# Handing every fourth product of a state-space scan from VectorE to GpSimd

## The chip, the cores and the metric

The kernel runs as one program on one core of a Trainium2 chip. The metric is the time of one execution on the device, in microseconds (us), as the median of several runs. In a profile PE is TensorE (PEld its weight loads), DVE is VectorE, ACT is ScalarE, POOL is GpSimd and SP is the queue that starts most transfers.

## What is computed

The whole program is a small network of four blocks. The change touches only the selective scan of the first block. There, after a convolution, every window's positions are walked in four directions, and a recurrence with 16 states runs along each walk:

```python
def step(h, inp):
    u, dt, Bl, Cl = inp
    dA = jnp.exp(dt[..., None] * A)
    h = h * dA + (dt * u)[..., None] * Bl[:, :, None, :]
    y = jnp.einsum('bkdn,bkn->bkd', h, Cl)
    return (h, y)
```

So for each of the 16 states there is a decay `exp(dt * A)`, an input `drive * B` with `drive = dt * u`, a scan over the positions, a product of the scanned state with `C`, and a sum of these products over the states.

## The kernel before

The scan stage takes the work in NU = 64 units: four groups of columns with 16 states (NS) each. A unit is one state on 128 partitions by UC = 1024 columns in f32. The columns hold 16 windows with L positions each. The first position of a window has decay zero, so one scan instruction runs through all windows of a unit. Each engine walks the units in order, in its own loop, and semaphores alone tie the loops together:

- TensorE, in iteration u: it waits for scan u-2 (`scanned`), spreads row n of `b_parts` over the partitions into `p_bb[:, u % 2]` (L510, two bf16 matmuls), waits until ScalarE has emptied `p_cb` (`c_copied`), spreads `c_parts` into `p_cb` (L516, two matmuls), and then adds `hc` of unit u-3 to `p_y` through an identity (L526, two f32 matmuls, four instructions).
- ScalarE: it waits for scan u-2, writes the decays into `d_a[:, u % 2]` (L539, an exponential), waits for `p_cb` and for `hc` of unit u-3, and copies `p_cb` to `cb` (L543).
- VectorE: it waits for the spread B, multiplies `drive` with `p_bb` in place in PSUM (L555), waits for the decays and for `hc` of unit u-3, and scans `d_a` (SBUF) and `p_bb` (PSUM) into `hs` (L560). After the scans of units 17, 33 and 49, and at the end, it reads the finished sum of a group from `p_y` (L550, `read_y`).
- GpSimd: it waits for scan u and the copied C and multiplies `hs` with `cb` into `hc` (L573).

`hs`, `cb` and `hc` are rings of three units (RING). `p_bb` and `d_a` have two slots each, `p_cb` has one, and each of them holds a whole unit. Together `p_bb` (4 banks), `p_cb` (2) and `p_y` (2) fill the PSUM. ScalarE's and VectorE's instructions run strictly in program order, and so do the instructions of TensorE, so a wait holds back all that stands behind it on its engine.

Of the kernel before, what the change touches and what calls it, by code (L numbers as in the profile page):

```python
# [8 lines left out]
ACT = mybir.ActivationFunctionType  # L9
ALU = mybir.AluOpType  # L10
# [11 lines left out]
L = NB * POS  # L22
RANK = 8
BANK = 512
# [33 lines left out]
def build_program(nc, io):  # L58
    with ExitStack() as ctx:
        sig = Signals(nc, ctx)  # L60
        chain_n = {"dve": 0, "act": 0, "pool": 0}

        def sb(name, shape, dt=F32, stack=ctx):
            return stack.enter_context(nc.sbuf_tensor(name, shape, dt))

        def ps(name, shape, dt=F32, stack=ctx):
            return stack.enter_context(nc.psum_tensor(name, shape, dt))
# [112 lines left out]
        with ExitStack() as st:  # L180
            x_tok = sb("x_tok", [128, T // 128, NB, C], stack=st)
            p_x = ps("p_x", [R, T], stack=st)
            with nc.Block() as block:
                @block.sync
                def _(sp):
                    sp.dma_start(ident[:], io["ident"]).then_inc(sig["load_const"], 16)
                    for b in range(NB):
                        sp.dma_start(x_tok[:, :, b, :], io["x"][b].rearrange("(j p) c -> p j c", p=128)).then_inc(sig["load_x"], 16)
                    sp.wait_ge(sig["load_const"], 16)
# [21 lines left out]
        with ExitStack() as st:  # L211
# [9 lines left out]
            drive = sb("drive", [128, 2, NW * L], stack=st)  # L221
            b_parts = sb("b_parts", [96, 2, NW * L], BF16, stack=st)
            c_parts = sb("c_parts", [96, 2, NW * L], BF16, stack=st)
            decay = sb("decay", [128, 2, NS], stack=st)
            pick = sb("pick", [96, NS, 128], BF16, stack=st)
# [260 lines left out]
            with ExitStack() as s2:  # L486
                UC = NW * L // 2
                RING = 3
                p_bb = ps("p_bb", [128, 2, UC], stack=s2)
                p_cb = ps("p_cb", [128, UC], stack=s2)  # L490
                p_y = ps("p_y", [128, UC], stack=s2)
                d_a = sb("d_a", [128, 2, UC], stack=s2)
                hs = sb("hs", [128, RING, UC], stack=s2)
                cb = sb("cb", [128, RING, UC], stack=s2)
                hc = sb("hc", [128, RING, UC], stack=s2)
                NU = 4 * NS
                def unit(u):
                    g, n = divmod(u, NS)
                    return g // 2, (g % 2) * UC, n
                with nc.Block() as block:  # L500
                    @block.tensor
                    def _(pe):
                        for u in range(NU + RING):
                            if u < NU:
                                k, c0, n = unit(u)
                                if u >= 2:
                                    pe.wait_ge(sig["scanned"], u - 1)
                                for h in range(2):
                                    c = slice(c0 + h * BANK, c0 + (h + 1) * BANK)
                                    last = pe.matmul(p_bb[:, u % 2, h * BANK:(h + 1) * BANK], pick[:, n], b_parts[:, k, c], start=True, stop=True)  # L510
                                last.then_inc(sig["b_spread"], 1)
                                if u >= 1:
                                    pe.wait_ge(sig["c_copied"], u)
                                for h in range(2):
                                    c = slice(c0 + h * BANK, c0 + (h + 1) * BANK)
                                    last = pe.matmul(p_cb[:, h * BANK:(h + 1) * BANK], pick[:, n], c_parts[:, k, c], start=True, stop=True)  # L516
                                last.then_inc(sig["c_spread"], 1)
                            if u >= RING:
                                v = u - RING
                                n = v % NS  # L520
                                if n == 0 and v:
                                    pe.wait_ge(sig["y_read"], v // NS)
                                pe.wait_ge(sig["hc"], v + 1)
                                for h in range(2):
                                    c = slice(h * BANK, (h + 1) * BANK)
                                    last = pe.matmul(p_y[:, c], ident[:], hc[:, v % RING, c], start=(n == 0), stop=(n == NS - 1))  # L526
                                last.then_inc(sig["y_summed"], 1)

                    @block.scalar
                    def _(act):  # L530
                        act.wait_ge(sig["first_decay_zero"], 1)
                        for u in range(NU):
                            k, c0, n = unit(u)
                            if u >= 2:
                                act.wait_ge(sig["scanned"], u - 1)
                            src = step[:, k, c0:c0 + UC].rearrange("p (w l) -> p w l", l=L)
                            dst = d_a[:, u % 2].rearrange("p (w l) -> p w l", l=L)

                            act.activation(dst[:, :, 1:L], src[:, :, 1:L], ACT.Exp, scale=decay[:, k, n:n + 1]).then_inc(sig["d_a"], 1)  # L539
                            act.wait_ge(sig["c_spread"], u + 1)  # L540
                            if u >= RING:
                                act.wait_ge(sig["hc"], u - RING + 1)
                            act.activation(cb[:, u % RING], p_cb[:], ACT.Copy).then_inc(sig["c_copied"], 1)  # L543

                    @block.vector
                    def _(dve):
                        def read_y(g):
                            k, c0, _ = unit(g * NS)
                            dve.wait_ge(sig["y_summed"], (g + 1) * NS)
                            dve.scalar_tensor_tensor(y_seq[:, k, c0:c0 + UC], seqf[:, k, c0:c0 + UC], skip[:, k:k + 1], p_y[:],  # L550
                                                     ALU.mult, ALU.add).then_inc(sig["y_read"], 1)
                        for u in range(NU):
                            k, c0, n = unit(u)
                            dve.wait_ge(sig["b_spread"], u + 1)
                            dve.tensor_tensor(p_bb[:, u % 2], drive[:, k, c0:c0 + UC], p_bb[:, u % 2], ALU.mult).then_inc(sig["d_bu"], 1)  # L555
                            dve.wait_ge(sig["d_a"], u + 1)
                            if u >= RING:
                                dve.wait_ge(sig["hc"], u - RING + 1)
                            dve.wait_ge(sig["d_bu"], u + 1)
                            dve.tensor_tensor_scan(hs[:, u % RING], d_a[:, u % 2], p_bb[:, u % 2], 0.0, ALU.mult, ALU.add).then_inc(sig["scanned"], 1)  # L560
                            if u >= NS and u % NS == 1:
                                read_y(u // NS - 1)
                        read_y(3)

                    @block.gpsimd
                    def _(pool):
                        pool.memset(d_a[:], 0.0).then_inc(sig["first_decay_zero"], 1)
                        for u in range(NU):
                            pool.wait_ge(sig["scanned"], u + 1)
                            pool.wait_ge(sig["c_copied"], u + 1)  # L570
                            if u >= RING:
                                pool.wait_ge(sig["y_summed"], u - RING + 1)
                            pool.tensor_tensor(hc[:, u % RING], hs[:, u % RING], cb[:, u % RING], ALU.mult).then_inc(sig["hc"], 1)  # L573

            with ExitStack() as s2:
# [104 lines left out]
def more(nc, io, loc):  # L681
# [613 lines left out]
    with ExitStack() as st:  # L1295
# [27 lines left out]
                 for t in range(4 * h, 4 * h + 4, n) for j in range(4)]  # L1323
        NU, EARLY = len(units), len(units) // 2
        scored = sb("scored", [128, EARLY, BANK], stack=st)
# [635 lines left out]
```

## Time and profile before

| | us |
|---|---|
| median of 3 runs (lowest, highest) | 1204.1 (1201.89, 1204.28) |
| profiled execution, its own time | 1202.41 |
| its span, first to last instruction | 1200.6 |
| the scan stage in it, first scan to end of last `read_y` | 97.65 to 332.36 |

The profiled execution takes 1.8 us more than its span, which lies outside the instructions, and is 1.7 us below the median. Times in the rows are microseconds from the start of the span.
### The profile page before, as it was taken

The page shows a single profiled execution, that of the slowest core. Times are in us where ns is not written, and L with a number is a line of the kernel's source. Part 1 is how long each engine was busy: PE and PEld are TensorE (multiplying, and loading weights), DVE is VectorE, ACT ScalarE, POOL GpSimd, SP SyncE. Part 2 cuts the span into 40 slices and gives each one's busy share as a digit, 9 for nine tenths or more (in the row PEclk, how much of TensorE's full clock was granted, in tenths as well). Part 3 has the DMA queues.
Part 4 walks back from the last instruction along what each step waited for, and adds up shares of the span by engine and source line. Part 5 has one row for each costly group of instructions (what it writes and reads, how often), then busy time and mean ns, then how long its engine had stood idle before and what let it go on. Part 6 is the DMA issues. An engine that isn't in the chain of part 4 may idle for free. (4 is left out here: it accounts for less than half of the span.)

```text
span 1200.6 us, 11335 instructions
## 1 busy us (share of the span) xinstructions
PE 747.2 (62%) x4114; PEld 435.2 (36%) x4114; DVE 479.7 (40%) x828; ACT 454.9 (38%) x1547; POOL 226.0 (19%) x130
## 2 busy tenths in 40 slices
PE   4807777777767655545555555557995555548975
PEld 1302222232233323223333333335773333325753
DVE  5597999999855534500000000012020000018652
ACT  3446556565424422033333333332212333335531
POOL 2276666666600000020000000000000000002200
PEclk9956999999995575555555555555555555555995
DMA  2020000000000000100000000000000000000000
GB/s 61 1 53 1 0 1 0 1 0 1 0 5 1 1 20 9 58 1 1 1 1 1 1 0 1 1 1 1 1 1 1 1 1 1 1 1 1 1 20 10
DMA packets 9570, 7.68 MB, mean 6 GB/s; under 512 B 7154, under 2 KB 8066, under 8 KB 9224
## 3 DMA queue, kind: packets, MB, share of 16 engines
q1 hardware_dynamic: 9512, 6.93, 2.4%
q8 instruction: 33, 0.54, 0.2%
q14 instruction: 25, 0.20, 0.1%
HBM read 5.09 MB, written 0.26 MB: 4 GB/s over the span
## 5 line engine op out<-in xcount | busy, mean ns | idle before, releaser
L791 PE MATMUL L2p_z<-L2yx,L2v 64*32 64x2 f32 x2048 | 267.9, 199 | 242.1 <-ACT L2yx L801 236.3
L801 ACT ACTIVATE L2yx<-L2p_z 32x2 f32<-32x2 f32 x1024 | 165.2, 161 | 389.2 <-PE L2p_z L791 389.2
L791 PEld LDWEIGHTS L2p_z<-L2yx,L2v 64*32 64x32 f32 x2048 | 180.4, 135 | 340.0 <-ACT L2yx L801 316.0
L692 DVE COPY xn<-L2yx 32x512 f32<-32x512 f32 x2 | 0.8, 417 | 431.1 <-ACT L2yx L801 264.2
L573 POOL TENSOR_TENSOR hc<-hs,cb 128x1024 f32<-128x1024 f32 x64 | 150.9, 2358 | 81.6 <-DVE hs L560 81.6
L560 DVE TENSOR_TENSOR_SCAN hs<-d_a,p_bb 128x1024 f32<-128x1024 f32 x64 | 146.3, 2286 | 8.9 <-ACT d_a L539 0.7
L526 PE MATMUL p_y<-hc,ident 128*128 128x512 f32 x256 | 122.5, 602 | 3.4 <-POOL hc L573 3.0
L1498 POOL COPY xo<-xn 64x256 f32<-64x256 f32 (+1 forms) x6 | 3.9, 691 | 555.9 <-DVE xn L157 555.9
L539 ACT ACTIVATE d_a<-step,decay 128x1016 f32<-128x1016 f32 x64 | 73.1, 1142 | 86.9 <-DVE hs L560 86.4
L510 PE MATMUL p_bb<-b_parts,pick 96*128 96x512 bf16 x128 | 40.5, 399 | 81.9 <-DVE hs L560 49.2
L555 DVE TENSOR_TENSOR p_bb<-drive,p_bb 128x1024 f32<-128x1024 f32 x64 | 77.3, 1207 | 6.2 <-PE p_bb L510 6.2
L543 ACT ACTIVATE cb<-p_cb 128x1024 f32<-128x1024 f32 x64 | 65.5, 1024 | 3.2 <-PE p_cb L516 3.1
L526 PEld LDWEIGHTS p_y<-hc,ident 128*128 128x128 f32 x256 | 48.7, 192 | 47.0 <-issue 31.6
L510 PEld LDWEIGHTS p_bb<-b_parts,pick 96*128 96x128 bf16 x128 | 7.8, 99 | 134.8 <-DVE hs L560 99.0
L516 PE MATMUL p_cb<-c_parts,pick 96*128 96x512 bf16 x128 | 39.9, 395 | 1.2 <-ACT cb L543 1.2
L1360 PE MATMUL atp_q<-kk,q 128*128 128x128 f32 x96 | 38.2, 502 | 0.0
L869 PE MATMUL L0p_z<-L0yx,L0v 64*32 64x64 f32 x192 | 30.2, 306 | 9.9 <-PEq L718 4.3
L1382 ACT ACTIVATE scored<-scored,anmx 128x256 f32<-128x256 f32 (+1 forms) x64 | 28.3, 442 | 17.2 <-DVE anmx L1375 17.1
L1626 PE MATMUL atp_o<-apt,vv 128*32 128x128 f32 x192 | 26.0, 282 | 2.3 <-ACT apt L1722 2.3
L869 PEld LDWEIGHTS L0p_z<-L0yx,L0v 64*32 64x32 f32 x192 | 17.6, 141 | 22.2 <-ACT L0yx L889 16.4
L889 ACT ACTIVATE L0yx<-L0p_z 32x64 f32<-32x64 f32 x96 | 20.1, 215 | 13.4 <-PE L0p_z L869 13.1
L1360 PEld LDWEIGHTS atp_q<-kk,q 128*128 128x128 f32 x96 | 24.0, 310 | 0.8
(387 smaller groups left out, 854.5 us busy)
## 6 DMA issues: line engine op xcount, KB each, us to landing
y_seq<-in_pick SPq DMA_DIRECT2D x1, 768.0 KB
b_parts<-part SPq DMA_DIRECT2D x3, 256.0 KB, 3.6
c_parts<-part SPq DMA_DIRECT2D x3, 256.0 KB, 4.4
pos<-in_pos SPq DMA_DIRECT2D x1, 512.0 KB, 3.6
ao<-in_at_o SPq DMA_DIRECT2D x1, 512.0 KB, 4.4
L1w<-in_L_w SPq DMA_DIRECT2D x1, 297.0 KB
L3w<-in_L_w SPq DMA_DIRECT2D x1, 297.0 KB
x_tok<-in_x SPq DMA_DIRECT2D x2, 128.0 KB, 2.8
```

The source lines that it names most:

```text
L510: last = pe.matmul(p_bb[:, u % 2, h * BANK:(h + 1) * BANK], pick[:, n], b_parts[:, k, c], start=True, stop=True)
L516: last = pe.matmul(p_cb[:, h * BANK:(h + 1) * BANK], pick[:, n], c_parts[:, k, c], start=True, stop=True)
L526: last = pe.matmul(p_y[:, c], ident[:], hc[:, v % RING, c], start=(n == 0), stop=(n == NS - 1))
L539: act.activation(dst[:, :, 1:L], src[:, :, 1:L], ACT.Exp, scale=decay[:, k, n:n + 1]).then_inc(sig["d_a"], 1)
L543: act.activation(cb[:, u % RING], p_cb[:], ACT.Copy).then_inc(sig["c_copied"], 1)
L555: dve.tensor_tensor(p_bb[:, u % 2], drive[:, k, c0:c0 + UC], p_bb[:, u % 2], ALU.mult).then_inc(sig["d_bu"], 1)
L560: dve.tensor_tensor_scan(hs[:, u % RING], d_a[:, u % 2], p_bb[:, u % 2], 0.0, ALU.mult, ALU.add).then_inc(sig["scanned"], 1)
L573: pool.tensor_tensor(hc[:, u % RING], hs[:, u % RING], cb[:, u % RING], ALU.mult).then_inc(sig["hc"], 1)
L791: pe.matmul(p_z[0:C, t % 2, 0:NB], v[:, 0:C], yx[:, NB * t:NB * (t + 1)], start=True, stop=True).then_inc(s("preact"), 1)
L801: act.activation(yx[0:C, NB * (t + 1):NB * (t + 2)], p_z[0:C, t % 2, 0:NB], ACT.Sigmoid).then_inc(s("state"), 1)
L869: pe.matmul(p_z[0:C, f, 0:NB * n], v[:, 0:C], by_batch[:, cols], start=True, stop=True).then_inc(s("preact"), 1)
L1360: return pe.matmul(dst[:, c:c + width], q[:, WITHIN[g], j, t * 128:(t + 1) * 128], kk[:, WITHIN[g], k0:k0 + width], start=True, stop=True)
```

## The change

Of every four units (SHARE) the last one, u % 4 == 3, is made differently. GpSimd multiplies its `drive` with its B. As it cannot read PSUM, B is spread into `p_cb` as an extra use of that tile, and ScalarE copies it to a new SBUF tile `d_bu` of two slots, where GpSimd multiplies in place. This is done three units ahead, at u % 4 == 0, behind that unit's own work on each of the three engines. The decays of such a unit are written by ScalarE into the unit's slot of `p_bb`, with an extra small copy of zeros for the first positions, so that its scan reads decays from PSUM and inputs from SBUF. TensorE also changes its order for all units: in iteration u it spreads B of unit u+1 first, then C of unit u, then does the sums of unit u-3.

```
+                d_bu = sb("d_bu", [128, 2, UC], stack=s2)
+                SHARE = 4
+                def on_pool(u):
+                    return u % SHARE == SHARE - 1
+                def cb_uses(u):
+                    return u + (u + SHARE - 1) // SHARE
...
TensorE:
+                        spread_b(0)
                         for u in range(NU + RING):
+                            if u + 1 < NU and not on_pool(u + 1):
+                                spread_b(u + 1)
                             if u < NU:
+                                spread_for_copy(u, c_parts, cb_uses(u))
                             if u >= RING:
...
                                 last.then_inc(sig["y_summed"], 1)
+                            if u < NU and u % SHARE == 0:
+                                spread_for_copy(u + SHARE - 1, b_parts, cb_uses(u) + 1)
ScalarE:
+                            dst = p_bb[:, u % 2].rearrange("p (w l) -> p w l", l=L) if on_pool(u) else zero
+                            if on_pool(u):
+                                act.activation(dst[:, :, 0:1], zero[:, :, 0:1], ACT.Copy).then_inc(sig["d_a_zero"], 1)
                             act.activation(dst[:, :, 1:L], src[:, :, 1:L], ACT.Exp, scale=decay[:, k, n:n + 1]).then_inc(sig["d_a"], 1)
...
+                            act.activation(cb[:, u % RING], p_cb[:], ACT.Copy).then_inc(sig["p_cb_read"], 1)
+                            if u % SHARE == 0:
+                                act.wait_ge(sig["p_cb_made"], cb_uses(u) + 2)
+                                if u >= 2 * SHARE:
+                                    act.wait_ge(sig["scanned"], u - SHARE)
+                                act.activation(d_bu_of(u), p_cb[:], ACT.Copy).then_inc(sig["p_cb_read"], 1)
VectorE:
+                            if not on_pool(u):
+                                dve.wait_ge(sig["b_spread"], spread_before(u) + 1)
+                                dve.tensor_tensor(p_bb[:, u % 2], drive[:, k, c0:c0 + UC], p_bb[:, u % 2], ALU.mult).then_inc(sig["d_bu"], 1)
...
+                                decays, inputs = p_bb[:, u % 2], d_bu_of(u)
...
+                            dve.tensor_tensor_scan(hs[:, u % RING], decays, inputs, 0.0, ALU.mult, ALU.add).then_inc(sig["scanned"], 1)
GpSimd, behind hc of unit u:
+                            if u % SHARE == 0:
+                                k, c0, n = unit(u + SHARE - 1)
+                                pool.wait_ge(sig["p_cb_read"], cb_uses(u) + 2)
+                                pool.tensor_tensor(d_bu_of(u), drive[:, k, c0:c0 + UC], d_bu_of(u), ALU.mult).then_inc(sig["d_bu_pool"], 1)
```

## Rows read from the trace of the kernel before

**Rows 1.** Busy time by engine (with counts), granted clock and DMA, over the scan stage.
```profile
97.65:332.36 234.71, 179.71 (x506) 68.46 (x506) 221.98 (x131) 134.41 (x127) 150.94 (x64) 0.98 0.00 0
```

**Rows 2.** The page's costliest groups: count, busy us, mean ns, idle before by releaser.
```profile
L573 POOL TENSOR_TENSOR hc<-hs,cb 128x1024 f32<-128x1024 f32 x64 | 150.9, 2358 | 81.6 <-DVE hs L560 81.6
```

**Rows 3.** Timeline of one unit in the steady part: start us, duration us, engine, line.
```profile
180.24 2.29 DVE L560 TENSOR_TENSOR_SCAN hs<-d_a,p_bb 128x1024 f32<-128x1024 f32 x1
...
182.45 1.21 DVE L555 TENSOR_TENSOR p_bb<-drive,p_bb 128x1024 f32<-128x1024 f32 x1
182.57 1.14 ACT L539 ACTIVATE d_a<-step,decay 128x1016 f32<-128x1016 f32 x1 [1.42 <-DVE hs L560]
...
182.59 0.60 PE L510 MATMUL p_bb<-b_parts,pick 96*128 96x512 bf16 x2 [0.79 <-DVE hs L560]
...
183.03 0.59 PE L516 MATMUL p_cb<-c_parts,pick 96*128 96x512 bf16 x2
...
183.46 1.88 PE L526 MATMUL p_y<-hc,ident 128*128 128x512 f32 x4
183.66 1.02 ACT L543 ACTIVATE cb<-p_cb 128x1024 f32<-128x1024 f32 x1
183.78 2.29 DVE L560 TENSOR_TENSOR_SCAN hs<-d_a,p_bb 128x1024 f32<-128x1024 f32 x1
...
185.99 1.21 DVE L555 TENSOR_TENSOR p_bb<-drive,p_bb 128x1024 f32<-128x1024 f32 x1
```

**Rows 4.** Timeline of the stage's start, where TensorE and ScalarE run back to back.
```profile
99.66 1.02 ACT L543 ACTIVATE cb<-p_cb 128x1024 f32<-128x1024 f32 x1
...
100.58 1.13 ACT L539 ACTIVATE d_a<-step,decay 128x1016 f32<-128x1016 f32 x1
...
109.10 0.59 PE L516 MATMUL p_cb<-c_parts,pick 96*128 96x512 bf16 x2
...
109.53 1.88 PE L526 MATMUL p_y<-hc,ident 128*128 128x512 f32 x4
109.73 1.02 ACT L543 ACTIVATE cb<-p_cb 128x1024 f32<-128x1024 f32 x1 [1.59 <-PE p_cb L516]
...
111.25 0.60 PE L510 MATMUL p_bb<-b_parts,pick 96*128 96x512 bf16 x2
```

**Rows 5.** Timeline of VectorE: the scan of unit 3.
```profile
108.22 2.29 DVE L560 TENSOR_TENSOR_SCAN hs<-d_a,p_bb 128x1024 f32<-128x1024 f32 x1
```

**Rows 6.** GpSimd's earlier product of half a unit: shortest, median and longest duration in ns.
```profile
L475 POOL TENSOR_TENSOR drive<-step,seq x4: 1256/1256/7061, 83.6 to 93.1; 128x512 f32<-128x512 f32 x4
```

**Rows 7.** Timeline of VectorE where a group's sum is read, after unit 17.
```profile
160.01 1.25 DVE L550 SCALAR_TENSOR_TENSOR y_seq<-seq,skip,p_y 128x1024 f32<-128x1024 f32 x1
...
161.18 1.22 DVE L555 TENSOR_TENSOR p_bb<-drive,p_bb 128x1024 f32<-128x1024 f32 x1
```

**Rows 8.** Timeline of TensorE at idle stretches (in brackets: how long, and what ended it).
```profile
61.05 1.07 PE L409 MATMUL p_bc<-seq,w_bc 128*64 128x512 f32 x2
...
103.51 1.03 PE L510 MATMUL p_bb<-b_parts,pick 96*128 96x512 bf16 x2 [1.63 <-DVE hs L560]
...
347.18 3.31 PE L614 MATMUL p_tr<-ident,y_tok 64*64 64x64 f32 x64 [3.93 <-DVE y_tok L647]
...
1143.22 0.65 PE L1613 MATMUL atp_t<-ident,scored 128*128 128x128 f32 x4 [2.00 <-DVE scored L1393]
```

**Rows 9.** Stretches around them, columns as in the first group; the clock stands third from last.
```profile
64.00:65.00 1.00, 0.00 (x0) 0.00 (x0) 1.00 (x3) 0.99 (x3) 0.14 (x1) 0.68 1.32 262
...
108.00:109.00 1.00, 1.00 (x3) 0.25 (x2) 0.87 (x2) 0.14 (x1) 1.00 (x1) 0.63 0.00 0
...
347.00:348.00 1.00, 0.82 (x22) 0.82 (x24) 0.93 (x3) 0.00 (x0) 0.00 (x0) 0.83 0.00 0
...
351.00:352.00 1.00, 0.90 (x2) 0.00 (x0) 0.42 (x1) 0.55 (x2) 0.00 (x0) 0.96 0.00 0
...
1141.00:1144.00 3.00, 0.88 (x6) 0.42 (x4) 2.86 (x16) 1.51 (x5) 0.00 (x0) 1.00 0.00 0
```

More of the change, by code:

```diff
@@ L495, in build_program, with spread_before, d_bu_of @@
                 hc = sb("hc", [128, RING, UC], stack=s2)
+                d_bu = sb("d_bu", [128, 2, UC], stack=s2)
                 NU = 4 * NS
+                SHARE = 4
+                def on_pool(u):
+                    return u % SHARE == SHARE - 1
+                def spread_before(u):
+                    return u - u // SHARE
+                def cb_uses(u):
+                    return u + (u + SHARE - 1) // SHARE
+                def d_bu_of(u):
+                    return d_bu[:, u // SHARE % 2]
                 def unit(u):
@@ L502, in _, with spread_b @@
                     def _(pe):
+                        def spread_b(u):
+                            k, c0, n = unit(u)
+                            if u >= 2:
+                                pe.wait_ge(sig["scanned"], u - 1)
+                            for h in range(2):
+                                c = slice(c0 + h * BANK, c0 + (h + 1) * BANK)
+                                last = pe.matmul(p_bb[:, u % 2, h * BANK:(h + 1) * BANK], pick[:, n], b_parts[:, k, c], start=True, stop=True)
+                            last.then_inc(sig["b_spread"], 1)
@@ new lines, in spread_for_copy @@
+                        def spread_for_copy(u, parts, uses):
+                            k, c0, n = unit(u)
+                            if uses:
+                                pe.wait_ge(sig["p_cb_read"], uses)
+                            for h in range(2):
+                                c = slice(c0 + h * BANK, c0 + (h + 1) * BANK)
+                                last = pe.matmul(p_cb[:, h * BANK:(h + 1) * BANK], pick[:, n], parts[:, k, c], start=True, stop=True)
+                            last.then_inc(sig["p_cb_made"], 1)
@@ L503, in _ @@
+                        spread_b(0)
                         for u in range(NU + RING):
+                            if u + 1 < NU and not on_pool(u + 1):
+                                spread_b(u + 1)
                             if u < NU:
[L505 to L517, printed above, removed]
+                                spread_for_copy(u, c_parts, cb_uses(u))
@@ L536, in _ @@
                             src = step[:, k, c0:c0 + UC].rearrange("p (w l) -> p w l", l=L)
-                            dst = d_a[:, u % 2].rearrange("p (w l) -> p w l", l=L)
+                            zero = d_a[:, u % 2].rearrange("p (w l) -> p w l", l=L)
+                            dst = p_bb[:, u % 2].rearrange("p (w l) -> p w l", l=L) if on_pool(u) else zero
+                            if on_pool(u):
+                                act.activation(dst[:, :, 0:1], zero[:, :, 0:1], ACT.Copy).then_inc(sig["d_a_zero"], 1)
                             act.activation(dst[:, :, 1:L], src[:, :, 1:L], ACT.Exp, scale=decay[:, k, n:n + 1]).then_inc(sig["d_a"], 1)
-                            act.wait_ge(sig["c_spread"], u + 1)
+                            act.wait_ge(sig["p_cb_made"], cb_uses(u) + 1)
                             if u >= RING:
                                 act.wait_ge(sig["hc"], u - RING + 1)
-                            act.activation(cb[:, u % RING], p_cb[:], ACT.Copy).then_inc(sig["c_copied"], 1)
+                            act.activation(cb[:, u % RING], p_cb[:], ACT.Copy).then_inc(sig["p_cb_read"], 1)
[4 more added lines that the diff above has]
+                                act.activation(d_bu_of(u), p_cb[:], ACT.Copy).then_inc(sig["p_cb_read"], 1)
                     @block.vector
@@ L553, in _ @@
                             k, c0, n = unit(u)
-                            dve.wait_ge(sig["b_spread"], u + 1)
-                            dve.tensor_tensor(p_bb[:, u % 2], drive[:, k, c0:c0 + UC], p_bb[:, u % 2], ALU.mult).then_inc(sig["d_bu"], 1)
+                            if not on_pool(u):
+                                dve.wait_ge(sig["b_spread"], spread_before(u) + 1)
+                                dve.tensor_tensor(p_bb[:, u % 2], drive[:, k, c0:c0 + UC], p_bb[:, u % 2], ALU.mult).then_inc(sig["d_bu"], 1)
                             dve.wait_ge(sig["d_a"], u + 1)
@@ L558, in _ @@
                                 dve.wait_ge(sig["hc"], u - RING + 1)
-                            dve.wait_ge(sig["d_bu"], u + 1)
-                            dve.tensor_tensor_scan(hs[:, u % RING], d_a[:, u % 2], p_bb[:, u % 2], 0.0, ALU.mult, ALU.add).then_inc(sig["scanned"], 1)
+                            if on_pool(u):
+                                dve.wait_ge(sig["d_a_zero"], u // SHARE + 1)
+                                dve.wait_ge(sig["d_bu_pool"], u // SHARE + 1)
+                                decays, inputs = p_bb[:, u % 2], d_bu_of(u)
+                            else:
+                                dve.wait_ge(sig["d_bu"], spread_before(u) + 1)
+                                decays, inputs = d_a[:, u % 2], p_bb[:, u % 2]
+                            dve.tensor_tensor_scan(hs[:, u % RING], decays, inputs, 0.0, ALU.mult, ALU.add).then_inc(sig["scanned"], 1)
                             if u >= NS and u % NS == 1:
@@ L569, in _ @@
                             pool.wait_ge(sig["scanned"], u + 1)
-                            pool.wait_ge(sig["c_copied"], u + 1)
+                            pool.wait_ge(sig["p_cb_read"], cb_uses(u) + 1)
                             if u >= RING:
```

## The prediction

> **What bounds the kernel now.** I read the page first for the stage, then the busy time over the stage, then the timeline of single units, and last the granted clock against TensorE's idle stretches. In the scan stage VectorE is busy 222.0 of 234.7 us, GpSimd 150.9, TensorE 179.7 and ScalarE 134.4 [rows 1]. The timeline of a unit shows why [rows 3]: a product starts at 182.45, its scan 1.33 us later, and the next product 2.21 us after that. The period is 3.54 us (185.99 - 182.45), all of it VectorE's. TensorE and ScalarE start their next unit when a scan ends, at 180.24 + 2.29 = 182.53: ScalarE 0.04 us later, TensorE 0.06 us later. Both are done before they are needed. Back to back TensorE needs 0.44 us for a spread of B, 0.43 for one of C [rows 3] and 1.72 for a sum (111.25 - 109.53) [rows 4], 2.59 us of each 3.54.
>
> **What the change takes away.** Call four units A, B, C, D, with D on GpSimd, and mark those of the four before with a prime. D loses its product, so a cycle of four costs VectorE 4 x 2.21 + 3 x 1.33 = 12.83 us instead of 14.16. Were VectorE still the bound, 16 cycles would save 21 us.
>
> **What it adds.** GpSimd gets a fifth product. Its nearest rows are the same operation on a whole unit, 2.36 us [rows 2], and that on half a unit, 1.26 us in median but 7.06 once [rows 6]. The longest stands where VectorE's loop has its own products with both inputs in SBUF (L455, L459 in the code); in the scan stage each VectorE instruction, the new scan included, has one SBUF input, so I take 2.36 (bounds 2.36 and 7.06). Five make 11.8 us in a cycle, under 12.83, and D's product begins behind A's `hc`, about three units ahead of its scan. It is hidden. The scan with operands swapped between memories has no row; both forms read one of each, so I take 2.29 (up to 0.1 more would be 1.6 us in all). The small copy of zeros has no row either: one column of each window, so between nothing and L539's 1.14 [rows 3], I take 0.2. It falls in D's part of the cycle, where ScalarE has over 1 us free, and costs nothing.
>
> **The new wait.** The extra B goes through `p_cb`, and ScalarE stands in its queue waiting for it, in front of the decays of unit B. This chain starts at the end of scan C', which TensorE awaits before it spreads B for A. Behind it TensorE does, back to back [rows 3, 4]: spread B for A (starts at +0.06), spread C for D' (+0.44), sum A' (+0.43), then 1.72 later spread B for unit B, spread C for A (+0.43), sum B' (+0.43), and 1.72 later the extra spread for D. That is 5.23 us. ScalarE can copy 0.63 after its start (109.73 - 109.10), its next instruction follows 0.92 after a copy (100.58 - 99.66) [rows 4], and the decays are ready after 1.14 + 0.03. So scan B starts 5.23 + 0.63 + 0.92 + 1.17 = 7.95 us after the end of scan C'. VectorE alone would be there at -0.08 + 2.21 (scan D') + 1.33 + 2.21 (unit A) + 1.33 = 7.00. The wait is 0.95 us in each cycle, which becomes 12.83 + 0.95 = 13.78 us: of 1.33 saved, 0.38 is left, 15 x 0.38 = 5.7 us. It is TensorE that paces the cycle now, which matters below.
>
> **The read of p_y.** The sum of unit 15 stood behind scan 16 and was early: `read_y` took 1.17 us of VectorE's time without a wait [rows 7]. Now it is in the iteration of unit C (18). Counted from the end of scan D', the extra copy ends at 4.67; spread C for B starts at 4.72, sum C' at 5.15, spread C for C at 6.87, sum D' at 7.30, and its result is there at 9.25 (start + 1.88 to 1.98). VectorE was free at 7.95. That is 1.3 us, three times: +3.9.
>
> **The start.** The clock is low there. Scan 1 waits for its decays behind the extra copy (in the place of the copy at 99.66, so 100.58 + 1.17 = 101.75 instead of 101.14, the scan of unit 3 less two periods [rows 4, 5]), and unit 3 saves 1.33: -0.7. But sum 0 now stands behind the spread of B for unit 4, which waits for scan 2, till 107.7. Before, TensorE's dense work began at 103.51 and the clock rose at 108.7 [rows 8, 9]. Now it begins about 4 us later, and spread, spread and sum (2.59 us) run at half rate first: +2.6. Together +1.9. At the end the `hc` of unit 63 waits behind that of 62 (2.36 against 2.21): +0.15.
>
> With an otherwise full clock this makes -5.7 + 3.9 + 1.9 + 0.15 = +0.3 us: a tie.
>
> **The clock.** In rows [rows 8, 9] TensorE stood idle from 62.12 and the clock fell at 64.4 (0.68 in that microsecond), after 2.2 us. It stood idle 3.9 us before 347.18, and the clock fell at 347.7. An idle stretch of 2.00 us (before 1143.22) did not lower it. The changed order makes two kinds of gaps. In each cycle TensorE ends sum D' at 9.2 and waits for scan C, which ends at 7.95 + 1.33 + 2.29 = 11.57: 2.4 us idle, where before it was 0.8 per unit [rows 3]. At a `read_y` it waits until 9.25 + 1.17 + 1.33 + 2.29 = 14.04: 4.9 us idle. The latter is longer than the stretch that lowered the clock, so I count three falls; the former lies between the rows on both sides, and I take two falls in the twelve other cycles (bounds none and eleven). A fall costs half of the time until the rise, as TensorE paces the cycle: 3.9 us from 347.18 to 351.1, 5.2 from 103.51 to 108.7, so 1.95 to 2.6, I take 2.2. Five falls are +11.
>
> The Trainium skill, TensorE: Matmul & The Clock Gate, section Why this matters for your kernels, also speaks against this change: it warns that a gap between bursts beyond a certain length brings the clock to half rate. By its limit the 4.9 us gaps would fall and the 2.4 us ones not, which would make the sum +7 instead of +11; this trace's fall after 2.2 us of idling does not agree with it.
>
> **Sum.** +0.3 + 11 = +11.3. On the profiled execution's 1202.4 us that is 1213.7, on the median 1204.1 it is 1215.4. I say 1215.
>
> **Rivals.**
> - The forecast, chance 0.50: three long falls and one to four short ones, 1204.1 + 0.3 + 2.2 x (4 to 7), so 1213 to 1220 (1209 to 1221 with the price of a fall at its ends).
> - Only the long gaps lower the clock, 0.15: +0.3 + 6.6, 1211. For it: the 2.00 us gap kept the clock. Against it: the fall at 64.4.
> - The clock holds from the first rise on, 0.13: +0.3, or -2 if it also rises as early as before: 1202 to 1204.4. For it: it held through the stage before (0.98 with the start) [rows 1], at gaps of 0.8 us. Against it: 4.9 us has no row in which it held.
> - Most cycles have a fall, 0.08: 10 or more, 1204.1 + 0.3 + 22 or above, 1224 to 1230.
> - The other side, 0.09: VectorE stays the bound and the kernel is faster. This is so if the decays of unit B come 0.95 us sooner, that is if the extra spread reaches ScalarE at 4.9 instead of 5.86 us. A sum's 1.72 or the 0.92 and 0.63 would have to be much shorter. If fully so, 16 x 1.33 - 3.9 - 0.15 = 17 us less: 1187; partly 1190 to 1200.
> - GpSimd's product or the new scan is dearer than its rows, 0.05: with 7.06 us for the product GpSimd has 4 x 2.36 + 7.06 = 16.5 us in a cycle and sets it: 15 x 2.3 = 35 us, 1238.
>
> For the last one the Trainium skill has a rule, SBUF — State Buffer, section Who interferes with whom: a VectorE instruction with two SBUF inputs contends with a GpSimd one that reads SBUF, one with a single SBUF input does not. The 7.06 us row agrees with the first half; by the second the product costs 2.36 here.
>
> **Range and chances.** A measurement of this kernel can tell about 0.2%, 2.4 us, from no change. Leaving out the faster case (0.09) and most of the two dearest (about 0.1) gives 1202 to 1223. Slower: 0.50 + 0.15 + 0.08 + 0.05, less a little of the forecast's foot, 0.74. Same: 0.13 and some of the neighbours, 0.14. Faster: 0.09 and the low end of the held clock, 0.12. The likeliest case's own range is 1209 to 1221.
>
> **What would show it.** Scan-to-scan times in a cycle of four: 2.21 into D, 3.54 for A, C, and 4.49 for B, with B's scan released by ScalarE's decays. A `read_y` released by TensorE's sum after 1.3 us. TensorE idle about 2.4 us once in each cycle and 4.9 us at three places, followed by a granted clock of 0.50 for some microseconds and a cycle of about 16 us. GpSimd busy 189 us with L573's mean unchanged. The prediction is wrong if the clock stays at 1.00 over the stage, or if scan B does not wait.

## The result and the profile after

The changed kernel took 1214.55 us (median of 4, 1212.62 to 1216.87) against 1204.19 before, a ratio of 1.0090 with a 95% interval of 1.0067 to 1.0112. So it is 10.4 us slower; 1215 was forecast. The profiled execution took 1214.75 us, its span is 1213.0 us.

First the busy time over the scan stage, with two stretches in which the granted clock fell and rose (columns as in [rows 1], which the first line answers):

```profile
98.61:344.97 246.36, 187.06 (x506) 73.72 (x506) 202.66 (x115) 144.54 (x159) 187.42 (x80) 0.91 0.00 0
168.00:169.00 1.00, 0.00 (x1) 0.01 (x1) 1.00 (x2) 0.00 (x0) 0.00 (x0) 0.92 0.00 0
169.00:172.00 3.00, 3.00 (x6) 1.42 (x7) 3.00 (x2) 1.08 (x2) 2.35 (x1) 0.50 0.02 5
172.00:173.00 1.00, 1.00 (x3) 0.29 (x2) 0.24 (x1) 0.97 (x1) 0.00 (x0) 0.88 0.00 0
```

VectorE lost the work that it should lose, 222.0 to 202.7 us, and the stage still grew from 234.7 to 246.4 us. The mean clock in it fell from 0.98 to 0.91. Another 1.0 us was there before the stage began (98.61 against 97.65); the change touches nothing there. Behind the stage the spans of all runs here differ by up to 4 us (868 to 872) though no edit touches anything there, so the experiments are also compared by their scan stages.

The timeline of a cycle of four at full clock, all engines but the weight loads (it answers to [rows 3]):

```profile
138.77 2.26 DVE L600 TENSOR_TENSOR_SCAN hs<-p_bb,d_bu 128x1024 f32<-128x1024 f32 x1
138.91 0.61 PE L523 MATMUL p_bb<-b_parts,pick 96*128 96x512 bf16 x2 [2.42 <-DVE hs L600]
...
142.29 2.29 DVE L600 TENSOR_TENSOR_SCAN hs<-d_a,p_bb 128x1024 f32<-128x1024 f32 x1
142.37 1.88 PE L549 MATMUL p_y<-hc,ident 128*128 128x512 f32 x4
...
144.09 0.60 PE L532 MATMUL p_cb<-b_parts,pick 96*128 96x512 bf16 x2
...
144.72 1.02 ACT L576 ACTIVATE d_bu<-p_cb 128x1024 f32<-128x1024 f32 x1 [1.13 <-PE p_cb L532]
145.64 1.13 ACT L567 ACTIVATE d_a<-step,decay 128x1016 f32<-128x1016 f32 x1
...
146.81 2.29 DVE L600 TENSOR_TENSOR_SCAN hs<-d_a,p_bb 128x1024 f32<-128x1024 f32 x1 [1.11 <-ACT d_a L567]
```

Read from the top: TensorE begins when scan C ends (136.57 + 2.29 = 138.86, which is also where scan D begins), after 2.42 us of idling. The extra spread for D starts at 144.09, that is 5.23 us after the end of scan C. ScalarE waits for it, copies at 144.72, makes the decays of B at 145.64, and only they release scan B at 146.81, 7.95 us after scan C. A cycle at full clock lasts 13.78 us, from a scan D at 138.77 to the next at 152.55, and eight of the fifteen cycles from unit 3 to unit 63 last that, or 16.30 with a `read_y` in them.

VectorE at the first read of `p_y` and in the cycle behind it (it answers to [rows 7]):

```profile
160.59 2.29 DVE L600 TENSOR_TENSOR_SCAN hs<-d_a,p_bb 128x1024 f32<-128x1024 f32 x1 [1.11 <-ACT d_a L567]
164.10 1.28 DVE L583 SCALAR_TENSOR_TENSOR y_seq<-seq,skip,p_y 128x1024 f32<-128x1024 f32 x1 [1.22 <-PE p_y L549]
...
173.00 2.29 DVE L600 TENSOR_TENSOR_SCAN hs<-d_a,p_bb 128x1024 f32<-128x1024 f32 x1 [0.76 <-ACT d_a L567]
...
178.48 2.29 DVE L600 TENSOR_TENSOR_SCAN hs<-d_a,p_bb 128x1024 f32<-128x1024 f32 x1 [2.07 <-POOL hc L613]
```

And TensorE there, and at the next short idle stretch (they answer to [rows 8]):

```profile
169.00 1.03 PE L523 MATMUL p_bb<-b_parts,pick 96*128 96x512 bf16 x2 [4.94 <-DVE hs L600]
...
184.37 0.60 PE L523 MATMUL p_bb<-b_parts,pick 96*128 96x512 bf16 x2 [2.42 <-DVE hs L600]
```

`read_y` waits 1.22 us for TensorE's sum. TensorE idles 4.94 us, the clock falls at 168.8, and it rises at 172.2. In that cycle the scan that waits longest is B's at 178.48, and it waits for GpSimd's `hc`, a wait that no cycle of 13.78 or 16.30 us has.

The waits over the stage, in us, times and longest:

```profile
POOL hc L613 <- PE p_y L549: 24.0, 22, 3.1
DVE hs L600 <- ACT d_a L567: 19.6, 17, 2.8
...
DVE hs L600 <- POOL hc L613: 13.1, 5, 3.3
DVE y_seq L583 <- PE p_y L549: 8.3, 4, 4.6
```

The clock fell six times in the stage. Three falls came inside the three idle stretches of 4.94 us, 4.8, 2.1 and 3.9 us after these began. The other three belong to three of the eleven stretches of 2.42 us: one came at 199.6, 0.3 us before its stretch ended, the others at 185.9 and 216.6, when TensorE had been at work again for 1.5 us.

### The profile page after: what moved, and what is told of

Same layout as the page of the kernel before. It is cut to its first block and busy times, and to the rows that moved or that the text cites. A ratio compares the mean times of both kernels' runs of the same rounds, so it can differ in the third digit from the quotient of the medians.

```text
span 1213.0 us, 11397 instructions
## 1 busy us (share of the span) xinstructions
PE 756.8 (62%) x4114; PEld 441.9 (36%) x4114; DVE 460.5 (38%) x812; ACT 465.0 (38%) x1579; POOL 262.6 (22%) x146
## 5 line engine op out<-in xcount | busy, mean ns | idle before, releaser
L835 PE MATMUL L2p_z<-L2yx,L2v 64*32 64x2 f32 x2048 | 269.2, 199 | 240.6 <-ACT L2yx L845 234.7
L835 PEld LDWEIGHTS L2p_z<-L2yx,L2v 64*32 64x32 f32 x2048 | 181.3, 136 | 338.9 <-ACT L2yx L845 314.9
L549 PE MATMUL p_y<-hc,ident 128*128 128x512 f32 x256 | 128.8, 628 | 1.3 <-POOL hc L613 1.3
L600 DVE TENSOR_TENSOR_SCAN hs<-d_a,p_bb 128x1024 f32<-128x1024 f32 x48 | 109.8, 2287 | 36.1 <-ACT d_a L567 19.6
L523 PE MATMUL p_bb<-b_parts,pick 96*128 96x512 bf16 x96 | 33.6, 439 | 77.9 <-DVE hs L600 45.4
L549 PEld LDWEIGHTS p_y<-hc,ident 128*128 128x128 f32 x256 | 51.2, 201 | 47.5 <-issue 36.0
L589 DVE TENSOR_TENSOR p_bb<-drive,p_bb 128x1024 f32<-128x1024 f32 x48 | 58.0, 1208 | 6.2 <-PE p_bb L523 6.2
L567 ACT ACTIVATE d_a<-step,decay 128x1016 f32<-128x1016 f32 x48 | 54.5, 1135 | 0.6 <-POOL d_a L607 0.6
L532 PE MATMUL p_cb<-c_parts,pick 96*128 96x512 bf16 x128 | 42.3, 415 | 10.4 <-ACT d_bu L576 9.3
L617 POOL TENSOR_TENSOR d_bu<-drive,d_bu 128x1024 f32<-128x1024 f32 x16 | 37.8, 2365 | 0.0
L600 DVE TENSOR_TENSOR_SCAN hs<-p_bb,d_bu 128x1024 f32<-128x1024 f32 x16 | 36.2, 2264 | 0.0
L532 PEld LDWEIGHTS p_cb<-c_parts,pick 96*128 96x128 bf16 x128 | 12.2, 105 | 38.8 <-ACT d_bu L576 17.3
```

Of the source, the lines that this page charges most:

```text
L600: dve.tensor_tensor_scan(hs[:, u % RING], decays, inputs, 0.0, ALU.mult, ALU.add).then_inc(sig["scanned"], 1)
L617: pool.tensor_tensor(d_bu_of(u), drive[:, k, c0:c0 + UC], d_bu_of(u), ALU.mult).then_inc(sig["d_bu_pool"], 1)
L835: pe.matmul(p_z[0:C, t % 2, 0:NB], v[:, 0:C], yx[:, NB * t:NB * (t + 1)], start=True, stop=True).then_inc(s("preact"), 1)
```

## Experiments

Each run was compared with the kernel before on the same chip, which took 1204.1 to 1204.4 us in each comparison. Where nothing else is said, the diff is against the changed kernel. All falls and rises of the clock are read from stretches of one microsecond.

**TensorE's old order, with the sharing.**

```
-                        spread_b(0)
                         for u in range(NU + RING):
-                            if u + 1 < NU and not on_pool(u + 1):
-                                spread_b(u + 1)
+                            if u < NU and not on_pool(u):
+                                spread_b(u)
```

> The sharing with GpSimd is kept, TensorE's old order is put back (B of unit u in iteration u, then C, then the sums, then the extra spread of B). Theory (the order makes the waits, the waits make TensorE idle, the idling lowers the clock): the extra spread now reaches ScalarE about 3.3 us after the end of scan C' (0.06 + 0.44 + 0.43 + 1.72 + 0.63) instead of 5.9, scan B does not wait, a cycle of four is 12.83 us, read_y does not wait, TensorE's longest idle stretch is about 1.7 us and the clock holds: 1204 - 20 = 1184. Rival (the sharing itself costs, by GpSimd's product or by the scan with its decays in PSUM): 1204 or above, with hc or the product longer than 2.36 us.

Measured: 1182.15 us, ratio 0.9825 (0.9805 to 0.9844). The timeline of a cycle, from scan D on:

```profile
120.12 2.26 DVE L599 TENSOR_TENSOR_SCAN hs<-p_bb,d_bu 128x1024 f32<-128x1024 f32 x1
...
123.49 1.02 ACT L575 ACTIVATE d_bu<-p_cb 128x1024 f32<-128x1024 f32 x1 [1.13 <-PE p_cb L532]
123.64 2.29 DVE L599 TENSOR_TENSOR_SCAN hs<-d_a,p_bb 128x1024 f32<-128x1024 f32 x1
124.41 1.13 ACT L566 ACTIVATE d_a<-step,decay 128x1016 f32<-128x1016 f32 x1
...
127.18 2.29 DVE L599 TENSOR_TENSOR_SCAN hs<-d_a,p_bb 128x1024 f32<-128x1024 f32 x1
...
130.72 2.29 DVE L599 TENSOR_TENSOR_SCAN hs<-d_a,p_bb 128x1024 f32<-128x1024 f32 x1
132.93 2.27 DVE L599 TENSOR_TENSOR_SCAN hs<-p_bb,d_bu 128x1024 f32<-128x1024 f32 x1
```

Here the copy for D starts 3.28 us after the end of scan C (117.92 + 2.29 = 120.21), the decays of B begin at 124.41, 2.8 us before their scan, and the cycle is 12.81 us. From the first rise of the clock on TensorE's longest idle stretch is 1.6 us, and the clock does not fall in the stage. The sharing by itself gives 22 us, 20.4 of them in the fifteen cycles (14.17 - 12.81). The new order takes all of it and 10 us more, 32.4 in all.

**The order alone.** All products on VectorE, the new order of TensorE:

```
                 def on_pool(u):
-                    return u % SHARE == SHARE - 1
+                    return False
...
                 def spread_before(u):
-                    return u - u // SHARE
+                    return u
...
                 def cb_uses(u):
-                    return u + (u + SHARE - 1) // SHARE
+                    return u
...
-                            if u < NU and u % SHARE == 0:
-                                spread_for_copy(u + SHARE - 1, b_parts, cb_uses(u) + 1)
```

and the same on ScalarE and GpSimd.

> TensorE's new order alone: all products on VectorE, no extra spread or copy, decays in SBUF for all units. Theory: the period stays 3.54 us, since the decays still come in time (2.05 + 1.17 = 3.2 us after scan u-1, wanted at 4.8). But read_y after unit 17 now waits for a sum that stands behind the spread of B for unit 19, which waits for scan 17: 2.9 us, three times, and TensorE then idles for about 5 us each time, so the clock falls three times: +9 for the waits and 2 to 6 for start and clock, 1214 to 1220. Rival (the order does no harm by itself, only with the sharing): 1204.

Measured: 1214.5 us, ratio 1.0089 (1.0072 to 1.0106). VectorE and TensorE at the first read:

```profile
163.34 1.28 DVE L576 SCALAR_TENSOR_TENSOR y_seq<-seq,skip,p_y 128x1024 f32<-128x1024 f32 x1 [2.85 <-PE p_y L549]
```

```profile
168.24 1.03 PE L523 MATMUL p_bb<-b_parts,pick 96*128 96x512 bf16 x2 [4.93 <-DVE hs L593]
```

Most cycles of four last 14.17 us, as before. The three with a read last 18.32 instead of 15.36: 2.96 us more each, 8.9 in all. The clock falls at all three reads and stays low for 6.8 us each time, but the cycle behind a read is only 0.4 to 0.55 us longer (14.56 to 14.72): where VectorE sets the pace a slow TensorE costs little. So the order alone costs as much as the whole change, by another sum: 8.9 for the waits, 1.5 behind the three falls and 0.2 at the start. And it costs 10 us without the sharing but 32 with it: the two parts of the change do not add up, because only with the extra B do the decays of a scan wait for TensorE.

**TensorE kept busy.** The waits stay, the idle stretches go. `keep_busy` spreads C of the unit into `p_cb` that many times, with no use, before the real spread:

```
                         for u in range(NU + RING):
+                            if u < NU - 1 and on_pool(u):
+                                keep_busy(u, 10 if u > NS and u % NS == 3 else 4)
                             if u + 1 < NU and not on_pool(u + 1):
                                 spread_b(u + 1)
```

> The changed kernel with its order and waits as they are, but TensorE repeats the spread of C for unit D 4 times (10 times after a read_y) in p_cb before it waits for scan C. The repeats are extra work without use. Theory (the clock): the waits of 0.95 and 1.3 us stay, no idle stretch of 2.4 or 4.9 us is left, the clock stays at 1.00 from its first rise on, every cycle is 13.78 us (16.3 with a read_y): 1202 to 1205. Rival (the waits alone make the loss, the clock is a by-product): 1213 or more, as the waits are the same and TensorE has more to do.

Measured: 1204.12 us, ratio 1.0002 (0.9992 to 1.0012). Busy time and clock from the first rise (111.9) to near the stage's end:

```profile
113.00:331.00 218.00, 198.73 (x638) 81.39 (x636) 188.48 (x107) 135.46 (x149) 177.96 (x76) 1.00 0.00 1
```

The clock is 1.00 throughout. VectorE's waits are unchanged:

```profile
162.91 1.28 DVE L593 SCALAR_TENSOR_TENSOR y_seq<-seq,skip,p_y 128x1024 f32<-128x1024 f32 x1 [1.22 <-PE p_y L559]
...
175.70 2.29 DVE L610 TENSOR_TENSOR_SCAN hs<-d_a,p_bb 128x1024 f32<-128x1024 f32 x1 [1.10 <-ACT d_a L577]
```

All cycles after the first are 13.78 or 16.30 us. With 156 more matmuls (in the stage 662 instead of 506) the kernel is 10 us faster. The scan stage takes 234.9 us, 11.5 less than the changed kernel's 246.4, and 11.3 of these are the six cycles with a fall. The clock is the whole difference between a tie and 10 us slower.

**The decays before the copy.** On top of the kernel kept busy, ScalarE copies the extra B behind the decays of unit B and in front of the wait for its C, no longer behind the copy of C of unit A:

```
+                            if u % SHARE == 1:
+                                act.wait_ge(sig["p_cb_made"], cb_uses(u - 1) + 2)
...
+                                act.activation(d_bu_of(u - 1), p_cb[:], ACT.Copy).then_inc(sig["p_cb_read"], 1)
...
-                            if u % SHARE == 0:
...
```

> The kernel e2_keep_busy (the clock held at 1.00 by useless repeats of a spread) with one line group moved on ScalarE: the copy of the extra B, and its wait, stand behind the decays of unit B, no longer in front of them. This prices the step of the new wait by itself. Theory: scan B no longer waits for decays, a cycle of four falls from 13.78 to VectorE's own 12.8 us, read_y keeps a wait: e2's 1204.1 less about 15 x 0.95 = 14, 1190. Rival (another wait of TensorE or GpSimd in the chain holds the cycle near 13.8 when this one is gone): 1200 or more.

Measured: 1191.64 us, ratio 0.9894 (0.9876 to 0.9911), 12.5 less than 1204.12. Cycles without a read are 12.81 us (12.92 for two early ones), so the wait of 0.95 was the only thing between 13.78 and VectorE's pace. Of the 12.2 us that the scan stage became shorter 2.7 lie in its start and first cycle, which is 14.27 us instead of 16.39. The cycles with a read became dearer than that, 16.62 us instead of 16.30, since the sum they wait for did not come earlier while VectorE did:

```profile
158.90 1.28 DVE L593 SCALAR_TENSOR_TENSOR y_seq<-seq,skip,p_y 128x1024 f32<-128x1024 f32 x1 [2.41 <-PE p_y L559]
```

**The reads one unit later.**

```
-                            if u >= NS and u % NS == 1:
+                            if u >= NS and u % NS == 2:
```

> The changed kernel with read_y one unit later (after units 18, 34, 50). Theory: its wait of 1.3 us and the 4.9 us idle stretches go, -3.9 us and three falls of the clock (some 6 us) less; the stretches of 2.4 us stay and lower the clock in some cycles still: 1203 to 1209. Rival (the three reads do not matter, the loss is spread over all cycles): 1212 to 1215.

Measured: 1210.90 us, ratio 1.0056 (1.0039 to 1.0072). The direction is right, the size missed: 3.7 us less than the change, not 5.5 to 11.5, and the intervals of the two ratios just overlap. In the scan stage it is 4.6 us less (241.7 against 246.4). The measured time lies between what the theory and what its rival gave. The waits at the reads and the 4.94 us stretches are gone, but the stretches of 2.42 us now lowered the clock seven times instead of three. The mean clock is again 0.91 (98.00 to 340.00):

```profile
98.00:340.00 242.00, 189.37 (x507) 73.68 (x508) 202.18 (x115) 144.35 (x159) 187.32 (x80) 0.91 0.00 0
```

How many of such stretches lower the clock could not be forecast from their length: three of eleven in the changed kernel, seven of fourteen here. What decides it was not tested.

**The decays in SBUF.** The kernel with the old order, and the scans of GpSimd's units read two SBUF inputs:

```
-                            dst = p_bb[:, u % 2].rearrange("p (w l) -> p w l", l=L) if on_pool(u) else zero
+                            dst = zero
...
-                                decays, inputs = p_bb[:, u % 2], d_bu_of(u)
+                                decays, inputs = d_a[:, u % 2], d_bu_of(u)
```

> The kernel e1_old_order with the decays of GpSimd's units in SBUF (d_a) as for all others, without the copy of zeros, so that the 16 scans of these units read two inputs from SBUF. Theory (such a VectorE instruction and a GpSimd one that reads SBUF hold each other up for their whole length, as the one 7.06 us product before suggests): GpSimd loses about 2.2 us in each cycle, 11.8 + 2.2 = 14.0 us against 12.8, so 15 x 1.2 = 18 us more, 1196 to 1204. Rival (where the decays lie makes no difference): 1182.

Measured: 1195.97 us, ratio 0.9929 (0.9911 to 0.9946), 14 us above the 1182.15 of the same kernel with decays in PSUM. Two groups of the stage by shape, one of each engine:

```profile
L609 POOL TENSOR_TENSOR hc<-hs,cb 128x1024 f32<-128x1024 f32 x64 | 180.4, 2844 | 5.8 <-DVE hs L596 5.8
...
L596 DVE TENSOR_TENSOR_SCAN hs<-d_a,d_bu 128x1024 f32<-128x1024 f32 x16 | 45.2, 2826 | 0.0
```

GpSimd's `hc` grew from 2.36 to 2.84 us in the mean over all 64, 30 us in all or 1.9 per such scan, and the scan itself from 2.26 to 2.83. A scan of this kind and the `hc` that started during it, each by itself:

```profile
147.57 3.02 DVE L596 TENSOR_TENSOR_SCAN hs<-d_a,d_bu 128x1024 f32<-128x1024 f32 x1
...
148.41 4.33 POOL L609 TENSOR_TENSOR hc<-hs,cb 128x1024 f32<-128x1024 f32 x1
```

An `hc` from 146.10 to 148.44 keeps its usual 2.34 us, and the scan that starts during it ends only 2.15 us after it. The next `hc` starts during the scan and ends 2.15 us after the scan. So in this trace whichever was first ran at its own speed and the other did its work behind it. Twelve of the sixteen scans took 3.0 us like this one. The other four, as at 162.33, began while GpSimd was idle and took 2.27, and only the `hc` begun in them was longer (4.25 us at 162.49). Of the 14 us 11.8 lie in the scan stage, 3.9 of them at its end, where GpSimd has fallen behind and the last sum is late. The theory took 2.2 us for what GpSimd loses, and the measured time is at the foot of its range. What the two engines do to each other here agrees with the rule of the Trainium skill, SBUF — State Buffer, section Who interferes with whom, that two SBUF inputs of a VectorE instruction contend with GpSimd's reads. The change avoids it by the decays in PSUM.

**Every third unit.** The kernel with the old order and SHARE = 3:

```
-                SHARE = 4
+                SHARE = 3
...
-                            if u < NU and u % SHARE == 0:
+                            if u + SHARE - 1 < NU and u % SHARE == 0:
```

> The kernel e1_old_order with SHARE = 3, every third unit on GpSimd. VectorE needs 3 x 2.20 + 2 x 1.33 = 9.3 us for three units, GpSimd 4 x 2.36 = 9.4 and some start latency, so GpSimd sets the pace at 9.45 to 9.6: 3.15 to 3.2 us for a unit against 3.20 with SHARE = 4. Theory (GpSimd is full, nothing to gain): 1179 to 1184, no difference that matters. Rival (an engine at its limit with a ring of three makes extra waits): 1186 or more.

Measured: 1203.45 us, ratio 0.9996 (0.9987 to 1.0006). A miss. The time lies in the rival's range, but neither mechanism was right: no ring held it up, the product for the third unit was late.

```profile
158.44 2.29 DVE L599 TENSOR_TENSOR_SCAN hs<-p_bb,d_bu 128x1024 f32<-128x1024 f32 x1 [1.34 <-POOL d_bu L616]
```

I had counted GpSimd's busy time and not the length of its chain: the product starts behind `hc` of a unit only two ahead. This wait comes 20 times, 24.9 us in all. The clock fell six times in this run too, five of them behind idle stretches of only 1.93 or 1.94 us, but the time for three units does not show it (10.70 to 10.73 us with and without a fall, 11.89 once with a read), since GpSimd and VectorE set the pace. So I turned GpSimd's order:

```
                         for u in range(NU):
+                            if u + SHARE - 1 < NU and u % SHARE == 0:
+                                k, c0, n = unit(u + SHARE - 1)
+                                pool.wait_ge(sig["p_cb_read"], cb_uses(u) + 2)
+                                pool.tensor_tensor(d_bu_of(u), drive[:, k, c0:c0 + UC], d_bu_of(u), ALU.mult).then_inc(sig["d_bu_pool"], 1)
                             pool.wait_ge(sig["scanned"], u + 1)
```

> The kernel e6_every_third with GpSimd's order turned: at every third unit it does the product for two units ahead first and hc of its own unit behind it. In e6 the product started only behind that hc, so it was ready 0.08 + 2.36 + 2.36 = 4.8 us after scan A, where the scan of the third unit wanted it after 3.46: 1.34 us of waiting each time. Theory (only the place in GpSimd's queue was wrong, GpSimd has the room): that wait goes, GpSimd's 9.4 us or VectorE's 9.3 set the pace of three units, 1178 to 1184. Rival (the product delays hc, and the ring of three makes scans and TensorE wait for it): 1186 to 1200.

Measured: 1180.22 us, ratio 0.9801 (0.9785 to 0.9818). VectorE's own timeline for three units:

```profile
126.41 2.29 DVE L599 TENSOR_TENSOR_SCAN hs<-d_a,p_bb 128x1024 f32<-128x1024 f32 x1
...
129.95 2.29 DVE L599 TENSOR_TENSOR_SCAN hs<-d_a,p_bb 128x1024 f32<-128x1024 f32 x1
132.16 2.26 DVE L599 TENSOR_TENSOR_SCAN hs<-p_bb,d_bu 128x1024 f32<-128x1024 f32 x1
...
135.67 2.29 DVE L599 TENSOR_TENSOR_SCAN hs<-d_a,p_bb 128x1024 f32<-128x1024 f32 x1
```

Three units take 9.26 us, VectorE's own sum of 3 x 2.20 + 2 x 1.33. It beats both kernels by 24 and 34 us. Against SHARE = 4 with the old order the two intervals overlap, so those 2 us are not settled. Two reads of `p_y` now wait, 1.29 and 1.66 us.

## Why the prediction was right, point by point

- **What it takes away and adds.** Right. GpSimd's product and the scan of a shared unit cost 2.365 and 2.264 us where 2.36 and 2.29 were taken; the copy of zeros took 0.2 us and is hidden. GpSimd's five products in a cycle fit under it (187.4 us busy in the stage, forecast 189).
- **The new wait.** Right to the hundredth: 7.95 us from scan C to scan B, 13.78 for a cycle. That this wait is all that separates the cycle from VectorE's pace was argued, and the run with the decays first shows it (12.81).
- **The read of p_y.** A wait of 1.22 us in the trace; a cycle with a read is 16.30 - 13.78 = 2.52 us longer, before it was 1.18: 3 x 1.34 = 4.0, forecast 3.9.
- **The start.** From the first scan to that of unit 3 the stage is 0.8 us shorter (9.81 against 10.57), forecast 0.7. The cycle behind it lasts 16.57 us, 2.8 more than 13.78, forecast 2.6. The clock rose at 114.2, 5.7 us after TensorE's dense work began at 108.56. In the run with the later reads, which has the same start, it rose 4.95 us after, and that cycle lasted 16.21: both are half of the time until the rise.
- **The clock.** Three falls at the reads as forecast, three at short stretches where two were taken. The six cycles with a fall are 1.53 to 2.86 us longer than those without (15.38, 15.48, 15.31, 17.99, 15.72, 16.64 against 13.78, or 16.30 with a read): 11.3 us, forecast 11. Kept busy, the kernel falls to 1204.1, so this term is the whole loss, and the other terms make the tie that was forecast (+0.3). The price of a fall was argued as half of the time in which TensorE works at half rate, and this holds for all six: 1.62, 1.71, 1.55, 1.71, 1.98 and 2.90 us by that rule, 1.60, 1.70, 1.53, 1.69, 1.94 and 2.86 in the cycles. The number of falls was in part a guess, as the prediction took two short ones between bounds of none and eleven. One fall more than taken and 0.3 us less for each nearly cancel, so it is partly luck that 11 met 11.3.
- **The sum of the trace.** -5.7 + 4.0 + 2.8 - 0.8 + 11.3 + 0.1 at the end is 11.7 us, and the stage is 11.65 us longer. The old order with the sharing accounts for the same terms from the other side. Its stage is 32.1 us shorter than the changed kernel's: 15 x 0.97 for the wait, 11.3 for the falls, 3 x 1.18 for the reads and 2.8 for the start make 32.2.
- **The range.** The prediction gives the likeliest case 1209 to 1221 with the price of a fall at its ends. Its own terms make 4 x 1.95 to 7 x 2.6, that is 1212 to 1223. The measured 1214.6 lies in both.

What was off is small. The path on which a fall is lost is not only the one I named. In the two cycles with the falls at 185.9 and 216.6 it is: the scan of B waits for its decays 1.70 us longer than in other cycles. In the other four cycles with a fall, and in the first cycle, the late sum of a unit holds back `hc` of three units later, and that holds back the scan of B (13.1 us in these five waits of scans for GpSimd). One cycle of each kind:

```profile
193.96 2.29 DVE L600 TENSOR_TENSOR_SCAN hs<-d_a,p_bb 128x1024 f32<-128x1024 f32 x1 [2.80 <-ACT d_a L567]
...
209.27 2.29 DVE L600 TENSOR_TENSOR_SCAN hs<-d_a,p_bb 128x1024 f32<-128x1024 f32 x1 [2.00 <-POOL hc L613]
```

Both start with TensorE's late work, so the price is the same. This is read from the traces; no run separates the two paths. The rule that only gaps beyond a certain length lower the clock, by which I had weighed a rival of +7, does not hold for this kernel as a sharp line: stretches of 2.42 us did it in three cases of eleven in the changed kernel and in seven of fourteen in the run with later reads.

## What to carry to other kernels

Sharing work out was sound; the reordering that came with it made a neighbour's queue the pace-setter. Before moving a step in one engine's program, walk one whole cycle through all queues and write down when and how long each engine is idle. Here TensorE set the pace, and a fall of the clock at an idle stretch of 2.4 or 4.9 us cost 1.5 to 2.9 us, more than the wait of 0.95 or 1.2 us beside it. Where VectorE or GpSimd set the pace, a fall cost 0.55 us at most. And an engine with room in busy time can still deliver late: check the chain from its input to the moment at which its result is wanted.

## What the runs showed of the hardware that was not expected

- The clock's fall is not settled by the length of an idle stretch alone. Of equal stretches of 2.42 us some lowered it and some did not, in the same run. With SHARE = 3 and the product behind, it fell five times behind stretches of 1.93 or 1.94 us. In the first of these TensorE was idle until 135.73 and at work again when the clock fell:

```profile
135.00:136.00 1.00, 0.27 (x2) 0.16 (x3) 0.67 (x1) 0.29 (x1) 1.00 (x1) 1.00 0.00 0
136.00:137.00 1.00, 1.00 (x5) 0.53 (x4) 0.00 (x0) 0.85 (x1) 1.00 (x2) 0.61 0.00 0
```

- A scan with one input in PSUM and the other in SBUF takes the same time whichever of them is which: 2.287 us and 2.264 to 2.291.
- The price of a fall was half of the time in which TensorE worked at half rate, in six of six falls of the changed kernel. How long the clock stays low is not all of it: at 4.94 us stretches it was low for 3.4, 6.8 and 6.8 us, partly while TensorE was idle, and the cycles lost 1.6, 1.9 and 2.9 us.
- A scan with both inputs in SBUF and a GpSimd product beside it did not share their time, they took turns: the one that started second ended 2.15 us after the first.
- Matmuls without any use can pay: 156 of them took 10 us off the changed kernel.
